# Attention stage: one loop over all 192 steps instead of eight units with a drain each, and the side work on other ticks

## The reference

```python
cq  = gelu(x @ wq + bq);   q_c = cq @ wqc + bqc;   q_r = rope(x @ wqr + bqr)
ckv = gelu(x @ wkv + bkv); k_c = ckv @ wkc + bkc;  k_r = rope(x @ wkr + bkr)
v = ckv @ wv + bv
q, k = gelu(concat(q_c, q_r)), gelu(concat(k_c, k_r))     # 16 heads of 16 channels
scores = q @ k.T / 4, causal;  attn = softmax(scores)
out = (attn @ v) @ wo + bo
```

## Time and profile before

| | us |
|---|---|
| median of 3 runs | 5210.27 (5207.43 to 5222.84) |
| profiled execution, span from first to last instruction | 5188.0 |
| attention stage, from its first loads to the last projection | 3703 to 4790 of the span |
| of it the main loop, from unit 0's first weights to unit 7's last | 3850.8 to 4767 |

### The profile page before, as it was taken

How to read it: one execution, slowest core, us unless ns; L and a number is a source line. 1 busy time by engine, 2 the same in 40 slices (tenths; PEclk the granted TensorE clock), 3 DMA queues, 4 the chain that set the end, 5 groups by cost and what they waited for, 6 DMA issues and landing times.

```text
span 5188.0 us, 49394 instructions
## 1 busy us (share of the span) xinstructions
PE 4001.8 (77%) x14866; PEld 2267.9 (44%) x14866; DVE 2848.7 (55%) x5588; ACT 2299.2 (44%) x4166; POOL 2537.2 (49%) x2184
## 2 busy tenths in 40 slices
PE   6888888769858878986778699769657777777892
PEld 2333333357625556762333366446422222233671
DVE  6999999741156663116888622263344445454432
ACT  5566656311167662114555333343335454545341
POOL 6999999622222333116888544334442323222356
PEclk9999999879978888997888799969767777788896
DMA  5656665412200002224555311232442222220245
GB/s 151 162 156 160 164 160 154 142 49 84 100 16 17 33 17 83 82 76 127 153 145 144 99 45 46 67 118 82 124 90 42 50 40 43 38 38 26 64 128 133
DMA packets 310700, 472.73 MB, mean 91 GB/s; under 512 B 34362, under 2 KB 167462, under 8 KB 310362
## 3 DMA queue, kind: packets, MB, share of 16 engines
q1 hardware_dynamic: 277008, 389.07, 27.5%
q0 software_dynamic: 29184, 76.12, 5.2%
q10 hardware_dynamic: 4224, 4.19, 0.2%
HBM read 375.46 MB, written 97.49 MB: 91 GB/s over the span
## 4 chain that ended last, share of the span: by engine, by line
PE 37%; POOL 8%; issue 5%; DVE 5%; ACT 5%; DMA 4%; SPq 1%; DVEq 0%; POOLq 0%; ACTq 0%
PE s_gate_up L2305 7%; PE s_result_sum L2321 4%; PE s_hidden_sum L1745 3%; PE s_result_sum L1756 3%; PE s_out_sum L3605 2%; POOL s_h L435 2%; PE s_scores_T L3592 2%; PE s_shared L2961 2%; PE s_scores L3556 2%; POOL s_gathered L1047 1%; PE s_shared L2971 1%; ACT s_weights_T L3411 1%; POOL s_h L444 1%; PE s_transposed L2295 1%; DMA parts_of_max<-s_max_parts 1%
## 5 line engine op out<-in xcount | busy, mean ns | idle before, releaser
L435 POOL TENSOR_TENSOR s_h<-s_dtu,s_bc 128x1024 f32<-128x1024 f32 x384 | 903.9, 2363 | 68.8 <-PE s_y_sum L477 54.7
L477 PE MATMUL s_y_sum<-s_h,identity 128*128 128x512 f32 x1536 | 773.1, 641 | 149.7 <-POOL s_h L444 136.4
L402 ACT ACTIVATE s_decay<-s_dt,s_A 128x512 f32<-128x512 f32 x768 | 498.3, 682 | 329.5 <-DVE s_h L377 322.7
L477 PEld LDWEIGHTS s_y_sum<-s_h,identity 128*128 128x128 f32 x1536 | 295.8, 203 | 589.8 <-issue 305.7
L3411 ACT ACTIVATE s_weights_T<-s_scores_T 128x1024 f32<-128x1024 f32 (+3 forms) x384 | 300.2, 812 | 408.1 <-PE s_scores_T L3592 406.8
L2305 PE MATMUL s_gate_up<-s_w_gate_up,s_rowsT 128*128 x1184 | 420.2, 487 | 2.4 <-issue 2.2
L3475 POOL TENSOR_SCALAR_AFFINE_SELECT s_weights_T<-s_weights_T 128x256 f32<-128x256 f32 x256 | 104.5, 411 | 627.9 <-ACT s_weights_T L3411 625.6
L444 POOL TENSOR_TENSOR s_h<-s_h,s_bc 128x512 f32<-128x512 f32 x288 | 367.3, 1276 | 25.2 <-DVE s_h L370 16.8
L2364 DVE TENSOR_TENSOR s_mid<-s_act,s_gate_up 128x128 f32<-128x128 f32 (+1 forms) x228 | 92.8, 407 | 451.9 <-ACT s_act L2337 451.9
L370 DVE TENSOR_TENSOR_SCAN s_decay<-s_decay,s_carry,s_h 128x512 f32<-128x512 f32 x240 | 303.4, 1278 | 25.0 <-POOL s_clip_flag L2633 14.5
L377 DVE TENSOR_TENSOR s_h<-s_decay,s_bc 128x512 f32<-128x512 f32 x480 | 313.0, 668 | 0.0
(11 more groups left out here) (521 smaller groups left out, 8097.5 us busy)
## 6 DMA issues: line engine op xcount, KB each, us to landing
s_bc<-s_bc_rows SPq DMA_DIRECT2D x384, 512.0 KB, 4.9
sorted_results<-s_result SPq DMA_DIRECT2D x160, 128.0 KB, 2.2
s_w_inter<-in_L_ffn_experts_inter SPq DMA_DIRECT2D x16, 1024.0 KB, 5.0
s_w_exp_out<-in_L_ffn_experts_out SPq DMA_DIRECT2D x16, 1024.0 KB, 8.1
s_queries<-parts_of_q SPq DMA_DIRECT2D x96, 128.0 KB, 4.9
s_keys<-parts_of_k SPq DMA_DIRECT2D x96, 128.0 KB, 8.0
results_by_token<-zeros SPq DMA_DIRECT2D x16, 512.0 KB, 5.8
s_pair<-results_by_token SPq DMA_DIRECT2D x16, 512.0 KB, 6.5
```

Source lines behind the costliest of these rows:

```text
L402: S.e.activation(self.decay[:, (2 * g + d) % 4, :], dt[q // self.passes % 2][:, at, :], ACT.Exp, scale=A[:, at, g % ns:g % ns + 1]).then_i ...
L435: G.e.tensor_tensor(self.h[r][:], dtu[q // self.passes % 2][:, at:at + 2, :], mid(self.bc[r][:, 0, :], 2), ALU.mult).then_inc(*self.fed.up())
L477: made = T.e.matmul(self.y[:, d, :], ident[:], self.h[r][:, d, :], start=False, stop=g % ns == ns - 1)
```

## The change

The loop goes on from unit to unit: `main` runs 24 steps per unit with a step number n from 0 to 191, and what it did in steps 24 to 26 (last product, transposes, division) is done in steps 0 to 2 of the next unit; after unit 7 one more pass does only that. A unit has 48 ticks, not 56. Then these ticks change:

- Maxima of `a` = 0: ticks 14 to 37 (before 20 to 43). Of `a` = 1: 20 blocks at ticks 38 to 47, 28 at ticks 0 to 13 of the next unit. So two blocks stand at every tick.
- `highest` of `a` = 0 at tick 39 (46), of `a` = 1 at tick 15 (18), and ahead of the maxima of its tick.
- SyncE: `stack_max(u + 1, 0)` goes ahead of `stage(u + 2)` and `stack(u + 2, 0)`.
- `values` at ticks 6, 7 (0, 1). TensorE waits for them before the first product of a unit, not before its first scores.
- Transposes 14, 15, 18, 19 (10, 11, 14, 15), latent 22, 28 (18, 20), `act` 30, 32 (22, 24), splits of even units three ticks later.
- The rope matmuls of q: ticks 44, 46 of the unit before (2, 4); of k: 20, 22 (26, 28); the swaps at 0 and 24 (6 and 30).
- Projection: pairs 0 and 1 in the odd unit itself at ticks 41 to 47, pairs 2 and 3 in the next unit at ticks 9 to 18; before all four at ticks 0 to 15 of the next. The bias goes to an even unit (ticks 8 to 14).

```diff
-    EARLY = 16
-    TICKS = 2 * NS + 8
-    ends = lambda s: 0 <= s < NS and STEPS[s][2] == 4 * STEPS[s][1] + 3
+    TICKS, N_STEPS = 2 * NS, n_units * NS
+    ends = lambda n: 0 <= n < N_STEPS and STEPS[n % NS][2] == 4 * STEPS[n % NS][1] + 3
+    group = lambda n: 4 * (n // NS) + 2 * STEPS[n % NS][0] + STEPS[n % NS][1]
-    FIRST = (20, 44)
-    score_tick = lambda a, i: FIRST[a] + i // 2 if a == 0 or i < EARLY else (i - EARLY) // 2
-    TURN, LATENT, ACTED, ROPE = ((10, 11), (14, 15)), (18, 20), (22, 24), ((2, 4), (26, 28))
-    OUT, MAX = 0, (46, 18)
+    FIRST = 14
+    at_tick = [FIRST + NS * a + NS * i // PER for a in range(2) for i in range(PER)]
+    EARLY = sum(t < TICKS for t in at_tick[PER:])
+    score_tick = lambda a, i: at_tick[PER * a + i] % TICKS
+    VALUES, TURN, LATENT, ACTED, ROPE = (6, 7), ((14, 15), (18, 19)), (22, 28), (30, 32), ((44, 46), (20, 22))
+    SWAP = (0, 24)
+    BIAS, OUT, MAX = (8, 10, 12, 14), ((41, 43), (44, 46), (9, 11), (13, 17)), (FIRST + 25, FIRST + 1)
...
+    def projects(u):
+        if u % DT:
+            return range(u // DT * PAIRS, u // DT * PAIRS + 2) if u > 0 else ()
+        return range(u // DT * PAIRS - 2, u // DT * PAIRS) if u > 0 else ()
+    def ropes(u, j):
+        made = u + (2 if j else 3)
+        return made if 0 < made < n_units and made % DT else 0
...
-            if 0 <= u < n_units:
+            if u >= 0:
                 main(u, beside)
...
             if u >= 0:
                 stack_max(u, 1)
+            if 0 <= u + 1 < n_units:
+                stack_max(u + 1, 0)
             if u + 2 < n_units:
                 stage(u + 2)
                 stack(u + 2, 0)
-            if 0 <= u + 1 < n_units:
-                stack_max(u + 1, 0)
...
         def main(u, beside):                              # TensorE
-            T.wait_ge(*value_here.at(2 * u + 1))
-            for s in range(NS + 3):
-                if s < NS:
+            for s in range(NS):
+                n = NS * u + s
+                if n < N_STEPS:
                     if s % (NS // 2) == 0:
                         T.wait_ge(*m_stacked[STEPS[s][0]].at(u))
-                    scores(u, s, 0)
+                    scores(n, 0)
                 beside(2 * s)
-                if s < NS:
-                    scores(u, s, 1)
-                if ends(s - 2):
-                    finish(u, s - 2)
+                if n < N_STEPS:
+                    scores(n, 1)
+                if ends(n - 2):
+                    finish(group(n - 2))
                 beside(2 * s + 1)
-                if 1 <= s <= NS:
-                    product(u, s - 1)
+                if 0 < n <= N_STEPS:
+                    product(n - 1)
```

More of the change, by code:

```diff
@@ L3108, in attention_stage @@
             pieces.append((1, 2, "bv"))
[L3109 to L3112, removed]
+        for t in projects(u):
+            pieces += [(k, k + 1, (n, t)) for n, k in zip(("turn out", "project"), OUT[t % PAIRS])]
         if 0 <= u + 1 < n_units:
-            pieces += [(i, i + 1, ("values", u + 1, i)) for i in range(2)]
+            pieces += [(k, k + 1, ("values", u + 1, i)) for i, k in enumerate(VALUES)]
         if 0 <= u + 2 < n_units and (u + 2) % DT == 0:
@@ L3126, in attention_stage @@
             pieces += [(score_tick(1, i), score_tick(1, i), ("scores", u + 1, 1, i)) for i in range(EARLY)]
-            pieces.append((MAX[0], MAX[0] + 1, ("max", u + 1, 0)))
-        B.place(pieces, [2 * s + 1 for s in range(NS + 3) if ends(s - 2)] if 0 <= u < n_units else [])
+        B.place(pieces, [2 * s + 1 for s in range(NS) if ends(NS * u + s - 2)])
     def program(main, **side):
@@ L3136, in program @@
                 work.append(("setup", 0))
-            if u >= DT and u % DT == 0:
-                work.append(("project", u // DT - 1))
+            if projects(u):
+                work.append(("project", projects(u)))
+            if 0 <= u < n_units and u % DT == 0:
+                work.append(("bias", u // DT))
             if 0 <= u + 1 < n_units:
@@ L3141, in program @@
             if 0 <= u + 2 < n_units:
-                work += [("front", u + 2), ("rope", u + 2), ("split", (u + 2, 0)), ("split", (u + 2, 1))]
+                work += [("front", u + 2), ("split", (u + 2, 0)), ("split", (u + 2, 1))]
+            for j in range(2):
+                if ropes(u, j):
+                    work.append(("rotate", (ropes(u, j), j)))
+            if ropes(u, 1):
+                work.append(("rope", ropes(u, 1)))
+            for a in (1, 0):
+                if 0 <= u + 1 - a < n_units:
+                    work.append(("highest", (u + 1 - a, a)))
             for a, late in ((1, True), (0, False), (1, False)):
@@ L3274, in highest, with project @@
             V.e.tensor_copy(mP[a][:, 2, :], mT[:]).then_inc(*max_split.up())
-        def project(b):
-            for j in range(PAIRS):
-                t = b * PAIRS + j
+        def project(pairs):
+            for t in pairs:
                 xt = X[:, 2 * t:2 * t + 2, :]
-                yield OUT + 4 * j + 3
+                yield OUT[t % PAIRS][1] + 1
                 V.wait_ge(*projected.at(t))
@@ L3393, in split, with project @@
                 S.e.activation(parts[n][:, i, :], act[ct][n][:], ACT.Copy).then_inc(*cast[n].up())
-        def project(b):
-            for j in range(PAIRS):
-                t = b * PAIRS + j
-                yield OUT + 4 * j + 1
+        def project(pairs):
+            for t in pairs:
+                yield OUT[t % PAIRS][0] + 1
                 S.wait_ge(*o_turned.at(t))
@@ L3467, in main @@
         def main(u, beside):
-            for s in range(NS + 3):
+            for s in range(NS):
+                n = NS * u + s
                 beside(2 * s)
-                if s < NS and diagonal(s):
-                    n, o = NS * u + s, max(0, STEPS[s][2] * P - STEPS[s][1] * CH)
+                if n < N_STEPS and diagonal(s):
+                    o = max(0, STEPS[s][2] * P - STEPS[s][1] * CH)
                     for pair in range(2):
@@ L3476, in main @@
                 beside(2 * s + 1)
-        program(main, combine=sums, front=front, rope=rope, split=split, project=project)
+        program(main, combine=sums, front=front, rope=rope, split=split, bias=bias)
     def tensor():
@@ L3564, in highest, with project @@
             T.e.transpose(f[0:NG * KT, 0:P], mn[a][:], K.ident[:]).then_inc(*mn_turned.up())
-        def project(b):
-            for j in range(PAIRS):
-                t = b * PAIRS + j
-                yield OUT + 4 * j
+        def project(pairs):
+            for t in pairs:
+                b, j = t // PAIRS, t % PAIRS
+                yield OUT[j][0]
                 T.wait_ge(*normalised.at(8 * (b + 1) - 2 + j // 2))
@@ L3584, in project, with scores @@
                 made.then_inc(*projected.up())
-        def scores(u, s, pair):
-            (hg, qh, kt), n = STEPS[s], NS * u + s
+        def scores(n, pair):
+            u, (hg, qh, kt) = n // NS, STEPS[n % NS]
             o = max(0, kt * P - qh * CH)
```

110 lines of the change are left out of this document (55 added, 55 removed).

## The result

The changed kernel takes 5173.91 us, median of 4 runs (5166.15 to 5178.56), beside 5208.85 for the kernel before (5199.17 to 5222.84, 4 runs): ratio 0.9933, 95% interval 0.9913 to 0.9954. That is 35 us less, where 109 were forecast. The direction was right, the size a third, and the time lies above the range. The profiled execution took 5166.15 us, its span is 5164.4.

The account below looks back on a forecast made before the run. No engine was taken as full: queue order and waits between engines set the attention stage's time. Savings of 47 + 54 + 0 + 8 + 0 = 109 us took 5210 to 5101, range 5050 to 5165.

Parts of the forecast that it names:

- (1): Boundaries between units: seven drains become ordinary steps, 73.5 us less, 47 left after moved work is charged; bounds 30 and 73.
- (4): Start of unit 0: its maxima are written at once, ahead of unit 1's transfers, 8 us less; bounds 3 and 12.
- even the old 9.6 would just fit: At the boundary: 9.8 us between split and next scores would cover even the maxima's old write and read, 9.6 us.
- (2): Steps 0 to 2: 106.4 us of excess goes, 52 returns with moved pieces, 54 us less; bounds 20 and 80.
- (3): Steps 3 to 22: same instructions on other ticks, 0 us, within 25 either way; VectorE's work does not change.
- (5): Tail: two of four projection pairs leave it, 7 us less, and cost the same in unit 7: 0.
- C: Boundary rival: maxima rows still come 5 us late each and PE cools again; 40 us less, 5170; chance 0.06.
- A: Clock rival: clock does not recover, or moved pieces stall the loop as before; 55 us less, 5155; chance 0.20.
- D: Slower rival: next maxima starve at tick 14 for keys or queries; 5241 at 20 us late per unit; chance 0.05.
- last sign of a wrong forecast: Middle steps of the units: the forecast is wrong if they grew by what the boundary gave back; no size given.

Follow-up runs that it names:

- e1: The kernel before, with only SyncE's write of the next unit's maxima moved ahead of the parts and 12 large reads: 5178.14 us, ratio 0.9948.
- e3: The changed kernel with SyncE's old order, the next unit's maxima behind the parts and 12 reads: 5216.93 us, ratio 1.0013 to the kernel before.
- e2: The changed kernel with the drain put back, each unit first ending the last group of the one before: 5161.49 us, ratio 0.9912 to the kernel before.
- e4: The changed kernel with the second chunk's layer norm statistics and factors at later ticks in even units: 5149.44 us, ratio 0.9889 to the kernel before.
- e13: e1 with the value matmuls moved from ticks 0 and 1 to ticks 16 and 17, which carry no maxima: 5128.02 us, ratio 0.9882.
- e15: The changed kernel with the 28 late blocks of maxima on ticks 0 to 5 and 10 to 13, clearing the values' ticks: 5141.86 us, ratio 0.991.
- e7: The changed kernel with every transposed score matmul issued twice: 5232.22 us, ratio 1.0047 to the kernel before.
- e12: The changed kernel with VectorE reducing only 128 columns of each block of maxima: 5112.35 us, ratio 0.9836 to the kernel before.

## Why the prediction was wrong in size

**(1) No drain, 47 us forecast.** The mechanism came: the steps 23 fell by 60.6 where I had 73.5 (4.6 each, not 2.8; they carry maxima, and rope of q or a projection pair), and PE no longer waits for the maxima's DMA. But the gain is the order of SyncE's queue (e1, e3), not the loop without a drain, which loses 12 us against one with it (e2; 6.6 by the loop). I had written the order off as a bonus of term (4) beside "even the old 9.6 would just fit".

**(2) Warm, empty starts, 54 us forecast.** This is the step that failed, with the price of the moved pieces in (1). The starts did fall, by 86.9 us of the 106.4 of excess. I had then charged 52 us for the pieces of (2) and 26 for those of (1), 78 in all. What stands against them is the rest of the sum: 915.5 less 73.5 and 106.4 is 735.6, the loop is 889.1, so 154 us, twice as much: 119 in steps 3 to 22, 20 in starts still above 9.4 us each, 13 in steps 23 and 2 in unit 7's last step. Not all of it is the pieces: the stall at tick 4, which I had not seen in the starts, is worth 20 us of loop (e4).

I took the pieces' prices from places where nothing stood behind them: a warm matmul, 1.16 us for eight, and 0.8 us for the bank. The values took 1.90 us a piece, and PE waited another 18.0 us over 14 pieces for ScalarE to read them, 1.3 each: 45 us, not 27. They had cost much the same where they stood, 2.06 us a piece and 16.1 us of waits in all, and with the same neighbours: two maxima per tick, in ticks 0 and 1 before and in 6 and 7 after, that share the three banks with them. PE waits until ScalarE has read a piece's bank, and loop and maxima stand behind. Among PE's waits in the loop of the kernel after are:

```profile
PE s_scores L3577 <- DVE s_max_parts L3295: 20.2, 11, 3.6
PE s_scores L3577 <- ACT s_straight L3378: 16.8, 6, 3.1
...
PE s_scores L3577 <- ACT s_values L3343: 9.6, 6, 1.6
PE s_scores L3577 <- ACT s_out_channels L3422: 8.3, 6, 1.6
PE s_misc L3577 <- ACT s_straight L3388: 7.6, 6, 1.3
PE s_scores L3577 <- ACT s_latent_qk L3371: 7.0, 4, 2.5
```

and before:

```profile
PE s_scores L3556 <- DVE s_max_parts L3274: 12.0, 7, 1.7
PE s_scores L3556 <- ACT s_latent_qk L3351: 11.3, 3, 3.8
PE s_scores L3556 <- ACT s_straight L3358: 9.3, 3, 3.1
PE s_misc L3556 <- ACT s_straight L3358: 7.4, 3, 2.5
```

Over all banks, and for all side pieces that ScalarE reads (`s_straight`, `s_values`, `s_latent_qk`, `s_out_channels`, `s_xT`), such waits are 77 us before and 97 after. In steps 3 to 22 they are 45 and 94: they moved with the pieces, and grew by 19. All those listed after are waits of L3577, the maxima, as is the one for the division (e2). I had seen maxima only as work of 0.67 us a step, from unit 6, where no piece meets them. e13 and e15 show the other side. On ticks without maxima the values keep 40 of the 56 us that they free (e13); where the maxima have to crowd on other ticks for it, 15 of 40 are left (e15).

**(3) Steps 3 to 22, 0 within 25.** The 119 us there hold the pieces of (1) and (2) too, and no run takes them apart from the rest, so this term can't be checked. "VectorE's work does not change" was true of its busy time and said nothing of its order.

**(4) SyncE's order at the start, 8 us.** Right: 7.9. **(5) Tail, 0.** It is 7.7 us shorter, and unit 7, which took two pairs, did not grow (57.0 us before, 56.5 after).

**The rivals.** The time lies 4 us above C (5170), so beyond A (5155) as well. Of A, "the moved pieces stall the loop as much as they did at the start" is what happened, and its clock too in part: low-clock time in the loop went from 387 us to 308, but in steps 3 to 22 it rose from 190 to 282; it moved with the pieces. In unit 0 the clock is 0.77 with no idle of PE over 4.03 us, in unit 7 it is 1.00 with the same banks. The Trainium skill, "TensorE: Matmul & The Clock Gate", section "A second HAM failure mode: psum-queue depth-cycling", would have the clock swing in such a loop without long gaps: units 0 to 5 agree (0.75 to 0.89, their longest idle 2.7 to 5.1 us), unit 7 does not (1.00, longest idle 1.3 us). C is false as a mechanism though its number is near, since no boundary waits for the rows. D did not occur: PE's list has no wait for keys or queries. My last sign of a wrong forecast, "steps in the middle that grew by what the boundary gave back", was the right one.

What stays open: how much of the 154 us is waiting for banks, how much the lower clock and how much the chain through VectorE. The sums over steps 3 to 22 set a bound: waits of all kinds are 44 of the 119 us there, and 75 are PE's own busy time, moved work and lower clock together. e7 and e12 move all three.

## What to carry to other kernels

A piece of side work has no price of its own: it costs what stands behind it on each in-order engine and in each shared bank while it waits to be read, so price it from a step that has the same neighbours, and look for ticks, or the cover of a drain, where no other user of its banks stands. When a loop's boundary is removed, count what its cover held; here a drain of 1.5 us was cheaper than what it hid. Put a small, urgent DMA ahead of large ones in its queue before touching anything else: that one move of two lines brought nearly all that the change brought.

## What the runs showed of the hardware

A small write to DRAM (32 rows of maxima) was through in 1.46 us with nothing ahead of it and in 6.93 us behind 12 transfers of 128 KB on the same queue (e3), much as in the earlier trace rows.

A 32x128 cast on VectorE, of the form that takes 0.21 us in the earlier trace rows, took 1.54 us in the kernel after. It ended at 3966.16, 0.08 us after a product of 2.12 us on GpSimd (3963.96 to 3966.08). It lengthens the split, and with it PE's wait for `s_max_parts`, which is part of what the moved split cost. It is no single case: of the 16 casts L3293 the eight that met such a product took 0.40 to 1.93 us and ended 0.07 to 0.08 us after it, and the other eight took 0.21 or 0.22. L3291, a cast of the same split that reads a PSUM bank, took 0.27 to 0.28 with a product beside it and without. No run moved the product away. The Trainium skill, "SBUF — State Buffer", section "Who interferes with whom", says that such a cast between SBUF tiles and a GpSimd operation can share a port pair that one of them holds for its whole instruction while the other waits; the trace agrees, with the 0.07 to 0.08 us between the two ends.

```profile
3964.62 1.54 DVE L3293 CAST s_max_parts<-s_max_rows 32x128 bf16<-32x128 f32 x1
```

```profile
3963.96 2.12 POOL L3477 TENSOR_TENSOR s_crossed<-s_crossed,s_parts_k 128x1024 f32<-128x1024 f32 x1 [1.20 <-ACT s_parts_k L3415]
```

A busier PE cost less than its length: 96 us more of busy time, with 42 us less of low clock (308 to 266), made the loop 64 us longer (e7).
